# Where the expert weights are kept, what SyncE stores first, and whether GpSimd scatters or gathers first, in a graph network followed by a mixture of experts

## The chip, the cores and the metric

The kernel runs on one core of a Trainium2 chip. The metric is the device time of one execution in microseconds (us), lower is better. Five engines work side by side: TensorE (PE; its weight loads are listed as PEld), VectorE (DVE), ScalarE (ACT), GpSimd (POOL) and SyncE (SP). They meet through semaphores. In this kernel SyncE starts all plain DMAs of the last stage, and GpSimd starts the indirect ones.

## The reference

The input is a graph with 3125 nodes of 256 channels and 53125 edges. A five-layer message network is applied to the normalised rows and added to them; then a mixture of 8 experts is applied to the normalised sum and added again. Cut to what matters here:

```python
x = x + mpnn(layernorm(x), edge_index, edge_attr, ...)      # 5 layers
h = layernorm(x)
logits = h @ Wg + bg + bias                                 # 8 experts
topk_vals, topk_idx = top_k(logits, 2)
w = softmax(topk_vals)                                      # two weights for each node
y[e] = relu(h @ W1[e] + b1[e]) @ W2[e] + b2[e]              # 256 -> 512 -> 256
x = x + sum over the two chosen e of w[e] * y[e]
```

## The kernel before

**Layers.** Nodes lie in 25 tiles of 125 (`NT`, `P`). The adjacency matrix stays in SBUF as fp8 blocks of 500 columns (`at_block(q)`, seven blocks). A layer multiplies its node products `m` with the blocks, first for one half of the channels (groups 0 to 6), then for the other (groups 7 to 13). After group 7 + q of the last layer, block q is not read again. `s_agg` counts the groups, `s_agge` their evictions, `s_tr` the row tiles that TensorE has transposed back (25 for each half of the channels), `s_lo` the row tiles that VectorE has added into the residual `x2`.

**Between the layers and the experts.** TensorE turns `x2` and forms the gate logits, VectorE forms the statistics and picks two experts for each node, ScalarE writes the normalised rows `xn`, SyncE stores them to `xn_dram`. VectorE then sorts the 6250 (node, expert) pairs by expert into tiles of 128 (`TT`), each expert's part filled up to whole tiles. `J` = 56 tiles always suffice; a tile beyond the last used one is a spare tile, whose rows go to the 128 padding rows behind the output. Tables from this: `rowG` (which rows to gather), `rowS` (which output rows to add to), `te` (the expert of a tile), `ts` (how many tiles have to be in memory before a tile may be added).

**The expert loop.** For each tile j, in this order of work: GpSimd gathers its rows from `xn_dram` into one of four buffers (`xtb`, `XB` = 4); TensorE transposes them (`rows`, L1562), ScalarE copies them to SBUF; TensorE multiplies with the up weights (`up`, L1571, 16 matmuls) that VectorE has copied from `w1s` into `w1c` (L1452); ScalarE applies relu; TensorE multiplies with the down weights in `w2s` (`down`, L1581, 8 matmuls); VectorE adds the bias from `b2B` (L1431) and scales with the pair's weight (L1437); GpSimd scatters the result with an accumulating DMA into the output (L1258). The output already holds the residual rows. A node is in two experts' tiles, so the first tile of an expert waits (`s_done`, counted by SyncE) until all tiles of the experts before it have landed. TensorE's order in step j is up of tile j+1, transposes of tile j+2, down of tile j. GpSimd's order is gather of tile j+4, scatter of tile j.

**Memory.** SBUF is laid out by hand in regions that overlap in time. `w1s` and `w2s` take 32 KB a partition each, `xn` 25 KB, `b2B` 8 KB. Before the change `xn` and `b2B` stand in the first adjacency blocks behind the residual, `w1s` where the products `m` were, and `w2s` where the hidden rows `hA` and `hB` were.

**SyncE's queue** runs in the order in which it is written, and each wait in it holds everything behind: residual inputs `x2`, `b2B`, `b1T` (eight DMAs of single values), `w1s`, `w2s`, the two stores of `xn`, the store of `x2` into the output, the zero padding rows; after that it counts landings.

Of the kernel before, what the change touches and what calls it, by code (L numbers as in the profile page):

```python
# [17 lines left out]
N = 3125  # L18
D = 256
E = 53125  # L20
L = 5
# [59 lines left out]
def gnn_ffn_program(nc, x, src, dst, edge_attr, mlp_w, mlp_b, ew1, ew2, bn_g, bn_b,  # L81
                    wg, bg, gbias, w1, b1, w2, b2, out):
    ctx = ExitStack()
    with ctx:
# [186 lines left out]
        assert r.at <= NT * 3 * CQ  # L271
        xn = r("xn", [TT, NT, XW], F32)
        b2B = r("b2B", [128, NE, D], F32)
        b1T = r("b1T", [128, NE, FK], F32)
# [6 lines left out]
        r = Region(hT_at)  # L281
        w2s = r("w2s", [128, NE, FK, D], F32)
        fmv = r("fmv", [P, NT, 2], F32)
# [33 lines left out]
        tsF = r("tsF", [1, J], F32)  # L317
        tsJ = r("tsJ", [1, J], F32)
        ts = r("ts", [1, J], I32)
        assert r.at <= dinvB_at + 2 * 4 * N  # L320
        r = Region(m_at)
        w1s = r("w1s", [128, NE, H, F], F32)
        xtb = r("xtb", [TT, XB, XW], F32)
# [179 lines left out]
        def node_rows(a, lo, hi):  # L503

            return a.rearrange("(t p) d -> p t d", p=P)[lo:hi, :, :]
# [670 lines left out]

        X_STORES = ((0, 13), (13, NT))
        EXP_AT = 10
        GATE, IDS, USED = (bank[4], bank[3]), bank[2], bank[3]
# [23 lines left out]
        def experts_sp(sp):  # L1203

            for n, t in enumerate(range(0, NT, X_PIECE)):

                sp.wait_ge(s_agg, H * NQ * (L - 1) + NQ + n + 1)
                some = slice(t, min(t + X_PIECE, NT))
                for lo, hi in SPANS:
                    sp.dma_start(x2[lo:hi, some, :], node_rows(x, lo, hi)[:, some, :]).then_inc(s_x2[n], 16)  # L1210
            sp.wait_ge(s_agg, L * H * NQ)
            sp.dma_start(b2B[:, :, :], b2.rearrange("(a e) f -> a e f", a=1).to_broadcast([128, NE, D])).then_inc(s_fw, 16)
            with nc.allow_non_contiguous_dma(reason="a few values for each hidden channel"):
                for e in range(NE):
                    sp.dma_start(b1T[:, e, :], b1[e:e + 1, :].rearrange("a (k p) -> p (a k)", p=128)).then_inc(s_fw, 16)

            sp.wait_ge(s_tr, NT * L)
            sp.dma_start(w1s[:, :, :, :].rearrange("p e k f -> p (e k) f"), w1.rearrange("e (k p) f -> p (e k) f", p=128)).then_inc(s_w1, 16)

            sp.wait_ge(s_tr, NT * (L + 1))  # L1220
            sp.dma_start(w2s[:, :, :, :].rearrange("p e k d -> p (e k) d"), w2.rearrange("e (k p) d -> p (e k) d", p=128)).then_inc(s_w2, 16)

            sp.wait_ge(s_wx, 1)
            for a, b in X_STORES:
                sp.wait_ge(s_fn, b)
                sp.dma_start(xn_dram.rearrange("(t p) d -> p t d", p=TT)[:, a:b, :], xn[:, a:b, :]).then_inc(s_xnd, 16)

            sp.wait_ge(s_lo, NT * (L + 2))
            for lo, hi in SPANS:
                sp.dma_start(node_rows(out[0:N, :], lo, hi), x2[lo:hi, :, :]).then_inc(s_res, 16)  # L1230
            sp.wait_ge(s_cst, 1)
            sp.dma_start(out[N:N + TT, :], zt[:, :]).then_inc(s_res, 16)

            sp.sem_inc(s_done, 1)
            for j in range(J):
                sp.wait_ge(s_acc[j % XB], 16 * (j // XB + 1))
                sp.sem_inc(s_done, 1)

        def experts_pool(pool, step):

            pool.wait_ge(s_cst, 2)
            pool.wait_ge(s_agg, H * NQ * L)
            pool.memset(xn[96:TT, :, :], 0.0).then_inc(s_cst, 1)  # L1243
# [8 lines left out]
            def accumulate(j):  # L1252

                before = pool.value_load(ts[0:1, j:j + 1], min_val=1, max_val=J + 1)
                pool.wait_ge(s_done, before)
                pool.wait_ge(s_yb, j + 1)
                pool.sem_inc(s_apart, 1)
                pool.indirect_dma_start(out[:, :], bass.IndirectOffsetOnAxis(ap=rowS[:, j:j + 1], axis=0), ytb[:, j % XB, :], None,  # L1258
                                        compute_op=ALU.add).then_inc(s_acc[j % XB], 16)
# [5 lines left out]
            pool.wait_ge(s_slot, 1)  # L1265
            for j in range(J):
                if j + XB < J:
                    pool.wait_ge(s_xtT, j + 1)
                    pool.wait_ge(s_sel, j + 1)
                    gather(j + XB)  # L1270
                accumulate(j)
            pool.wait_ge(s_done, J + 1)
# [42 lines left out]
        def experts_dve(dve, step, rounded, inverse_root):  # L1315
# [100 lines left out]
            step(dve.tensor_reduce(tsF[:, :], cmpJ[:, 0, :, :], axis=XYZ, op=ALU.add))  # L1416
            step(dve.scalar_tensor_tensor(tsJ[:, :], teF[:, :], NE - 0.5, iotaJ[0:1, :], ALU.is_gt, ALU.mult))
            step(dve.tensor_tensor(tsF[:, :], tsF[:, :], tsJ[:, :], ALU.max))
            step(dve.tensor_scalar(ts[:, :], tsF[:, :], 1.0, None, ALU.add))
# [42 lines left out]
            dve.wait_ge(s_slot, 1)  # L1462
            dve.wait_ge(s_w1, 16)
            weights_of(0, 0, None)
# [9 lines left out]
        def experts_pe(pe):  # L1474
# [79 lines left out]
            pe.wait_ge(s_slot, 1)  # L1554
            pe.wait_ge(s_w1, 16)
            pe.wait_ge(s_w2, 16)
# [688 lines left out]
```

## Time and profile before

| | us |
|---|---|
| median of 3 runs | 1569.53 (1569.2 to 1570.07) |
| the profiled execution | 1569.19 |
| its span, first to last instruction | 1567.5 |
| TensorE busy (matmuls) | 1402.3 (89%) |
| VectorE busy | 718.3 (46%) |
| ScalarE busy | 421.6 (27%) |
| GpSimd busy | 179.4 (11%) |
| mean granted clock of TensorE | 0.948 of full speed |

Rows of a timeline give start and duration in us, engine, line, operation, what it writes and reads, and in brackets how long the engine had been idle and who ended that. SPq is SyncE issuing a DMA. A row of the chain of waits gives start, duration and what the end of the program was waiting for then. A row of windows gives the stretch, its length, the busy time of each engine with its count of instructions, the granted clock, the DMA share and GB/s. Times run from the start of the span.

### The profile page before, as it was taken

The page shows a single profiled execution, that of the slowest core. Times are in us where ns is not written, and L with a number is a line of the kernel's source. Part 1 is how long each engine was busy: PE and PEld are TensorE (multiplying, and loading weights), DVE is VectorE, ACT ScalarE, POOL GpSimd, SP SyncE. Part 2 cuts the span into 40 slices and gives each one's busy share as a digit, 9 for nine tenths or more (in the row PEclk, how much of TensorE's full clock was granted, in tenths as well). Part 3 has the DMA queues.
Part 4 walks back from the last instruction along what each step waited for, and adds up shares of the span by engine and source line. Part 5 has one row for each costly group of instructions (what it writes and reads, how often), then busy time and mean ns, then how long its engine had stood idle before and what let it go on. Part 6 is the DMA issues. An engine that isn't in the chain of part 4 may idle for free.

```text
span 1567.5 us, 25937 instructions
## 1 busy us (share of the span) xinstructions
PE 1402.3 (89%) x9117; PEld 859.2 (55%) x9118; DVE 718.3 (46%) x1713; ACT 421.6 (27%) x1159; POOL 179.4 (11%) x156
## 2 busy tenths in 40 slices
PE   2666468988888999999999999999999998899996
PEld 1655344444444554446444474444644466799995
DVE  6789777777743332313223141221312238444442
ACT  1820344433340330103101040010401025344342
POOL 1000100000000000000000000000000010577774
PEclk9976689999999999999999999999999998999998
DMA  5244000000000000000000000000000329444443
GB/s 118 69 155 172 1 1 1 1 2 1 1 21 1 14 1 1 0 1 14 1 0 0 1 15 0 0 1 7 2 0 11 72 49 326 90 71 70 68 73 44
DMA packets 49739, 58.01 MB, mean 37 GB/s; under 512 B 14432, under 2 KB 41789, under 8 KB 49372
## 3 DMA queue, kind: packets, MB, share of 16 engines
q1 hardware_dynamic: 38876, 41.78, 9.1%
q0 software_dynamic: 10752, 14.74, 6.0%
q8 instruction: 70, 1.15, 0.3%
q14 instruction: 41, 0.34, 0.1%
HBM read 42.42 MB, written 14.09 MB: 36 GB/s over the span
## 4 chain that ended last, share of the span: by engine, by line
PE 80%; DVE 7%; ACT 6%; issue 3%; DMA 2%; DVEq 1%; SPq 1%; POOL 0%; POOLq 0%; ACTq 0%
PE bank L937 43%; PE bank L1027 9%; PE bank L1571 6%; PE bank L1581 6%; PE bank L843 5%; PE bank L2187 4%; ACT at L2055 2%; PE bank L2129 2%; DMA xin<-in_x 1%; PE bank L943 1%; PE bank L2185 1%; DVE ohL L1844 1%; PE bank L1562 1%; ACT xjunk L2002 1%; ACT xjunk L1995 1%
## 5 line engine op out<-in xcount | busy, mean ns | idle before, releaser
L937 PE MATMUL bank<-at,m 125*128 125x500 fp8e4 (+1 forms) x3500 | 688.3, 354 | 7.8 <-issue 4.1
L937 PEld LDWEIGHTS bank<-at,m 125*128 125x128 f16 x3500 | 317.7, 98 | 369.0 <-issue 50.7
L953 DVE SCALAR_TENSOR_TENSOR aggT<-bank,dnL,dinvB 128x500 f32<-128x500 f32 (+1 forms) x56 | 38.2, 682 | 453.8 <-PE bank L943 453.8
L1571 PEld LDWEIGHTS bank<-xtT,w1c 128*128 128x128 f32 x896 | 109.6, 193 | 3.3 <-ACT xtT L1293 0.5
L1571 PE MATMUL bank<-xtT,w1c 128*128 128x128 f32 x896 | 110.0, 276 | 0.1
L1581 PE MATMUL bank<-w2s,h1T 128*128 x448 | 106.0, 380 | 0.0
L1258 POOL DMA_INDIRECT out_rows<-ytb,rowS x56 | 98.0, 1750 | 49.2 <-issue 18.2
L1243 POOL MEMSET xn<- 32x6450 f32 x1 | 5.5, 5473 | 792.8 <-PE bank L943 792.8
L1049 ACT ACTIVATE hB<-aggT,prm 128x500 f32<-128x500 f32 (+1 forms) x28 | 18.7, 667 | 267.1 <-DVE aggT L1099 267.1
L1581 PEld LDWEIGHTS bank<-w2s,h1T 128*128 128x128 f32 x448 | 80.8, 190 | 8.9
L2044 ACT ACTIVATE encI<-bank 125x500 int32<-125x500 f32 x32 | 18.8, 587 | 228.5 <-PE bank L2191 228.4
L2187 PE MATMUL bank<-cnt,ohS 128*128 128x250 bf16 x504 | 75.8, 297 | 0.0
L1951 DVE TENSOR_TENSOR cnt<-iotaK,nowKD 128x2000 bf16<-128x2000 int16 x63 | 75.1, 1192 | 0.0
L1299 ACT ACTIVATE h1T<-bank,b1T 128x128 f32<-128x128 f32 x224 | 64.0, 368 | 27.6 <-issue 23.0
L1250 POOL DMA_INDIRECT xtb<-xn_dram,rowG x56 | 57.2, 1022 | 66.8 <-DVE rowG L1413 45.6
L1027 PE MATMUL bank<-hB,wt 128*128 128x500 f32 (+1 forms) x140 | 64.7, 544 | 0.0
L2185 PE MATMUL bank<-ohD,now 128*12 128x50 bf16 x504 | 25.0, 192 | 44.1 <-DVE ohS L1953 43.5
L869 DVE SCALAR_TENSOR_TENSOR m<-bank,dinvP,m 125x256 f16<-125x256 f32 x100 | 43.0, 478 | 35.5 <-ACT m L864 35.4
L1452 DVE COPY w1c<-w1s 128x1024 f32 x56 | 39.8, 711 | 41.8 <-issue 23.8
L2055 ACT ACTIVATE at<-encB 125x500 fp8e4<-125x500 uint8 (+1 forms) x96 | 57.0, 599 | 0.4 <-DVE encB L1916 0.4
L2185 PEld LDWEIGHTS bank<-ohD,now 128*12 128x12 bf16 x504 | 19.1, 101 | 65.6 <-issue 65.1
L2187 PEld LDWEIGHTS bank<-cnt,ohS 128*128 128x128 bf16 x504 | 47.2, 104 | 11.7
(387 smaller groups left out, 1649.4 us busy)
## 6 DMA issues: line engine op xcount, KB each, us to landing
slrow<-sl_dram SPq DMA_DIRECT2D x26, 512.0 KB, 5.0
w1s<-in_L_ffn_W SPq DMA_DIRECT2D x1, 4096.0 KB, 14.5
w2s<-in_L_ffn_W SPq DMA_DIRECT2D x1, 4096.0 KB, 19.1
xin<-in_x SPq DMA_DIRECT2D x1, 2800.0 KB
out_rows<-x SPq DMA_DIRECT2D x1, 2800.0 KB
x<-in_x SPq DMA_DIRECT2D x2, 1344.0 KB
xn_dram<-xn SPq DMA_DIRECT2D x1, 1677.0 KB, 7.5
dinvB<-dinv_dram SPq DMA_DIRECT2D x1, 1562.5 KB
```

The source lines that it names most:

```text
L843: last = pe.matmul(pair_slot(t), half_in(l, h)[:, t * P:(t + 1) * P], wb[:, l % 2, h, :], start=h == 0 and t % 2 == 0, stop=h == H - 1 and ...
L937: pe.matmul(agg_bank(l, g)[:, 0:w], m[:, s, k, h * 128:(h + 1) * 128], at_block(q)[:, s, :], start=s == 0 and k == 0, stop=False)
L1027: last = pe.matmul(lin_bank(l, j, q)[:, 0:w], weights, src_k, start=k == 0, stop=k == ks[-1])
L1250: pool.indirect_dma_start(xtb[:, j % XB, :], None, xn_dram[:, :], bass.IndirectOffsetOnAxis(ap=rowG[:, j:j + 1], axis=0)).then_inc(s_xt[j ...
L1258: pool.indirect_dma_start(out[:, :], bass.IndirectOffsetOnAxis(ap=rowS[:, j:j + 1], axis=0), ytb[:, j % XB, :], None, compute_op=ALU.add). ...
L1299: last = act.activation(h1T[:, u, k, :], bank[4 + u][:, k * TT:(k + 1) * TT], ACT.Relu, bias=b1T[:, bass.ds(e, 1), k:k + 1].rearrange("p a ...
L1571: last = pe.matmul(bank[4 + u][:, k * TT:(k + 1) * TT], w1c[:, u, h, k * 128:(k + 1) * 128], xtT[:, u, h, :], start=h == 0, stop=h == H - 1)
L1581: last = pe.matmul(bank[6 + u][:, 0:D], h1T[:, u, k, :], w2s[:, bass.ds(e, 1), k, :].rearrange("p a f -> p (a f)"), start=k == 0, stop=k = ...
L1951: dve.tensor_tensor(cnt1[side][:, :, :, :], to_all(iotaK[:, :, :], U // 2), by_pairs(nowKD[:, side, 0, :], GW), ALU.is_equal)
L2055: last = act.activation(at_block(q)[:, field:field + FIELDS * (GROUPS - 1) + 1:FIELDS, a:a + n], byte[:, f, :, 0:n], ACT.Copy, saturate=False,
L2185: pe.matmul(sums_w, now[:, side, 0:12, j], ohD[side][:, j // 2, :, j % 2], start=False, stop=False)
L2187: last = pe.matmul(out_w, ohS[side][:, j // 2, :, j % 2], cnt1[side][:, j // 2, :, j % 2].rearrange("p (g n) -> p g n", g=GROUPS), start=F ...
```

## The change

It has four parts.

1. Memory and loads. `w1s` moves into the adjacency region, behind `x2`, and is loaded in three pieces (experts 0 and 1, 2 to 4, 5 to 7), each when the last layer has used block 2, 3 or 4 for the last time. `w2s` moves to the place of `m` and is loaded after the last aggregation. `xn` and `b2B` move to the place of `hA` and `hB`; so GpSimd's clearing of the padding rows of `xn` waits for all row transposes, and `b2B` is loaded after the last eviction.
2. Stores. SyncE stores the residual rows and the zero padding rows ahead of the two stores of `xn`.
3. Spare tiles. Two VectorE operations go, which had made each spare tile wait for all tiles ahead of it. A spare tile now waits for all tiles of all experts.
4. GpSimd's loop. Scatter j stands ahead of gather j+4.

```diff
         assert r.at <= NT * 3 * CQ
-        xn = r("xn", [TT, NT, XW], F32)
-        b2B = r("b2B", [128, NE, D], F32)
+        w1s_at = r.at
+        w1s = r("w1s", [128, NE, H, F], F32)
...
         r = Region(hT_at)
-        w2s = r("w2s", [128, NE, FK, D], F32)
+        xn = r("xn", [TT, NT, XW], F32)
+        assert r.at >= dinvB_at
+        b2B = r("b2B", [128, NE, D], F32)
...
         r = Region(m_at)
-        w1s = r("w1s", [128, NE, H, F], F32)
+        w2s = r("w2s", [128, NE, FK, D], F32)
...
+        W1_PIECES = ((2, 0, 2), (3, 2, 5), (4, 5, NE))
...
-            sp.wait_ge(s_agg, L * H * NQ)
-            sp.dma_start(b2B[:, :, :], b2.rearrange("(a e) f -> a e f", a=1).to_broadcast([128, NE, D])).then_inc(s_fw, 16)
+            for block, a, b in W1_PIECES:
+                assert w1s_at + 4 * H * F * b <= NT * CQ * (block + 1)
+                sp.wait_ge(s_agg, H * NQ * (L - 1) + NQ + block + 1)
+                sp.dma_start(w1s[:, a:b, :, :].rearrange("p e k f -> p (e k) f"), w1[a:b].rearrange("e (k p) f -> p (e k) f", p=128)).then_inc(s_w1, 16)
             with nc.allow_non_contiguous_dma(reason="a few values for each hidden channel"):
                 for e in range(NE):
                     sp.dma_start(b1T[:, e, :], b1[e:e + 1, :].rearrange("a (k p) -> p (a k)", p=128)).then_inc(s_fw, 16)
 
+            sp.wait_ge(s_agg, L * H * NQ)
             sp.wait_ge(s_tr, NT * L)
-            sp.dma_start(w1s[:, :, :, :].rearrange("p e k f -> p (e k) f"), w1.rearrange("e (k p) f -> p (e k) f", p=128)).then_inc(s_w1, 16)
-
-            sp.wait_ge(s_tr, NT * (L + 1))
             sp.dma_start(w2s[:, :, :, :].rearrange("p e k d -> p (e k) d"), w2.rearrange("e (k p) d -> p (e k) d", p=128)).then_inc(s_w2, 16)
+
+            sp.wait_ge(s_agge, L * H * NQ)
+            sp.dma_start(b2B[:, :, :], b2.rearrange("(a e) f -> a e f", a=1).to_broadcast([128, NE, D])).then_inc(s_fw, 16)
+            sp.wait_ge(s_cst, 1)
+            sp.dma_start(out[N:N + TT, :], zt[:, :]).then_inc(s_res, 16)
+            sp.wait_ge(s_lo, NT * (L + 2))
+            for lo, hi in SPANS:
+                sp.dma_start(node_rows(out[0:N, :], lo, hi), x2[lo:hi, :, :]).then_inc(s_res, 16)
 
             sp.wait_ge(s_wx, 1)
             for a, b in X_STORES:
                 sp.wait_ge(s_fn, b)
                 sp.dma_start(xn_dram.rearrange("(t p) d -> p t d", p=TT)[:, a:b, :], xn[:, a:b, :]).then_inc(s_xnd, 16)
 
-            sp.wait_ge(s_lo, NT * (L + 2))
-            for lo, hi in SPANS:
-                sp.dma_start(node_rows(out[0:N, :], lo, hi), x2[lo:hi, :, :]).then_inc(s_res, 16)
-            sp.wait_ge(s_cst, 1)
-            sp.dma_start(out[N:N + TT, :], zt[:, :]).then_inc(s_res, 16)
...
             pool.wait_ge(s_cst, 2)
-            pool.wait_ge(s_agg, H * NQ * L)
+            pool.wait_ge(s_agge, H * NQ * L)
+            pool.wait_ge(s_tr, NT * (L + 1))
             pool.memset(xn[96:TT, :, :], 0.0).then_inc(s_cst, 1)
...
             for j in range(J):
+                accumulate(j)
                 if j + XB < J:
                     pool.wait_ge(s_xtT, j + 1)
                     pool.wait_ge(s_sel, j + 1)
                     gather(j + XB)
-                accumulate(j)
...
-            step(dve.scalar_tensor_tensor(tsJ[:, :], teF[:, :], NE - 0.5, iotaJ[0:1, :], ALU.is_gt, ALU.mult))
-            step(dve.tensor_tensor(tsF[:, :], tsF[:, :], tsJ[:, :], ALU.max))
             step(dve.tensor_scalar(ts[:, :], tsF[:, :], 1.0, None, ALU.add))
...
-            dve.wait_ge(s_w1, 16)
+            dve.wait_ge(s_w1, 16 * len(W1_PIECES))
...
-            pe.wait_ge(s_w1, 16)
+            pe.wait_ge(s_w1, 16 * len(W1_PIECES))
             pe.wait_ge(s_w2, 16)
```

GpSimd at the start of the expert loop, before: the clearing of `xn`, the four first gathers, then the gather of tile 4 ahead of the scatter of tile 0 (L1250 is a gather, L1254 the reading of `ts`, L1258 a scatter).

```order
L1243 MEMSET xn 32x6450 [waits s_agg,s_cst]
L1250 DMA xtb<-xn_dram,rowG 128x258 [waits s_xnd,s_tab]
L1250 DMA xtb<-xn_dram,rowG 128x258 x3
L1250 DMA xtb<-xn_dram,rowG 128x258 [waits s_xtT,s_sel,s_slot,s_res,s_tab]
L1254 TENSOR_LOAD ts
L1254 ISA x2
L1258 DMA out_rows<-ytb,rowS 3253x256 [waits s_done,s_yb]
L1250 DMA xtb<-xn_dram,rowG 128x258 [waits s_xtT,s_sel]
```

The same place of the changed kernel, where the gather is L1255 and the scatter L1263.

```order
L1248 MEMSET xn 32x6450 [waits s_tr,s_agge,s_cst]
L1255 DMA xtb<-xn_dram,rowG 128x258 [waits s_xnd,s_tab]
L1255 DMA xtb<-xn_dram,rowG 128x258 x3
L1259 TENSOR_LOAD ts [waits s_slot,s_tab,s_res]
L1259 ISA x2
L1263 DMA out_rows<-ytb,rowS 3253x256 [waits s_done,s_yb]
L1255 DMA xtb<-xn_dram,rowG 128x258 [waits s_xtT,s_sel]
```

The first scatter, with its waits for a tile's result and for the residual rows, has moved ahead of the fifth gather, and so for every later pair.

SyncE from the last load of `x2` (named x_156 here) to the end, before.

```order
L1210 DMA x_156<-in_x 13x256
L1212 DMA b2B<-in_L_ffn_b 128x2048 [waits s_agg]
L1215 DMA b1T<-in_L_ffn_b 128x4x1 x8
L1218 DMA w1s<-in_L_ffn_W 128x16x512 [waits s_tr]
L1221 DMA w2s<-in_L_ffn_W 128x32x256 [waits s_tr]
L1226 DMA xn_dram<-xn 128x13x258 [waits s_fn,s_wx]
L1226 DMA xn_dram<-xn 128x12x258 [waits s_fn]
L1230 DMA out_rows<-x_156 112x25x256 [waits s_lo]
L1230 DMA out_rows<-x_156 13x25x256
L1232 DMA out_rows<-zt 128x256 [waits s_cst]
```

And in the changed kernel.

```order
L1212 DMA x_156<-in_x 13x256
L1216 DMA w1s<-in_L_ffn_W 128x4x512 [waits s_agg]
L1216 DMA w1s<-in_L_ffn_W 128x6x512 [waits s_agg] x2
L1219 DMA b1T<-in_L_ffn_b 128x4x1 x8
L1223 DMA w2s<-in_L_ffn_W 128x32x256 [waits s_tr,s_agg]
L1226 DMA b2B<-in_L_ffn_b 128x2048 [waits s_agge]
L1228 DMA out_rows<-zt 128x256 [waits s_cst]
L1231 DMA out_rows<-x_156 112x25x256 [waits s_lo]
L1231 DMA out_rows<-x_156 13x25x256
L1236 DMA xn_dram<-xn 128x13x258 [waits s_fn,s_wx]
L1236 DMA xn_dram<-xn 128x12x258 [waits s_fn]
```

The up weights have moved ahead of all else in three pieces, `b2B` behind the down weights, and the residual's stores ahead of those of `xn`.

## Rows read from the trace of the kernel before

**Rows 1.** The page, chain that ended last, by engine, whole span.

```profile
PE 80%; DVE 7%; ACT 6%; issue 3%; DMA 2%; DVEq 1%; SPq 1%; POOL 0%; POOLq 0%; ACTq 0%
```

**Rows 2.** Chain of waits, 1327 to 1382: start, duration, what.

```profile
1333.02 8.14 DMA xtb<-xn_dram,rowG
...
1341.30 0.67 PE bank L1562 x2
...
1342.51 4.79 PE bank L1571 x32
...
1379.11 1.78 PE bank L1571 x16
```

**Rows 3.** Timeline, expert loop, 1377 to 1389: tile 8 and the tiles around it.

```profile
1377.22 1.89 PE L1581 MATMUL bank<-w2s,h1T 128*128 x8
...
1379.91 0.35 DVE L1437 TENSOR_SCALAR ytb<-ytt,wS 128x256 f32<-128x256 f32 x1 [0.22 <-DVE ytt L1431]
...
1380.95 1.89 PE L1581 MATMUL bank<-w2s,h1T 128*128 x8
1381.10 1.92 POOL L1258 DMA_INDIRECT out_rows<-ytb,rowS  x1 [0.96 <-issue]
...
1383.32 0.99 POOL L1250 DMA_INDIRECT xtb<-xn_dram,rowG  x1 [0.30 <-issue]
...
1384.46 0.38 PE L1562 MATMUL bank<-ident,xtb 128*128 128x128 f32 x2
...
1384.68 1.89 PE L1581 MATMUL bank<-w2s,h1T 128*128 x8
```

**Rows 4.** Scatters: ns min/median/max, 1352 to 1545; group with mean, 1360 to 1540.

```profile
L1258 POOL DMA_INDIRECT out_rows<-ytb,rowS x52: 1583/1694/2078, 1351.1 to 1541.6; - x52
...
L1258 POOL DMA_INDIRECT out_rows<-ytb,rowS x49 | 86.3, 1761 | 32.2 <-issue 16.6 <-PE bank L1562 8.4 <-DVE wS L1445 7.3
```

**Rows 5.** Gathers into xtb, 1340 to 1420: from issue to landing.

```profile
DMA to landing us min/median/max: 2.8/2.8/3.7
```

**Rows 6.** Timelines of GpSimd (first, last of eight wide spacings) and VectorE (last result).

```profile
1388.46 1.96 POOL L1258 DMA_INDIRECT out_rows<-ytb,rowS  x1 [0.46 <-issue]
...
1393.51 1.59 POOL L1258 DMA_INDIRECT out_rows<-ytb,rowS  x1 [1.79 <-DVE wS L1445]
...
1552.49 1.55 POOL L1258 DMA_INDIRECT out_rows<-ytb,rowS  x1 [1.97 <-DVE ytb L1437]
...
1553.08 0.57 DVE L1437 TENSOR_SCALAR ytb<-ytt,wS 128x256 f32<-128x256 f32 x1
1557.03 1.55 POOL L1258 DMA_INDIRECT out_rows<-ytb,rowS  x1 [2.98 <-SPq L1237]
```

**Rows 7.** Timeline of SyncE, 1262 to 1350.

```profile
1282.24 6.52 SPq L1215 DMA_DIRECT2D b1T<-in_L_ffn_b  x8
...
1321.39 10.18 SPq L1230 DMA_DIRECT2D out_rows<-x  x2
```

**Rows 8.** Windows: length, busy PE, PEld, DVE, ACT, POOL, granted clock, DMA share, GB/s.

```profile
1297.00:1305.00 8.00, 7.96 (x72) 7.73 (x71) 5.06 (x41) 4.34 (x12) 0.00 (x0) 0.91 1.07 374
...
1313.00:1317.00 4.00, 2.00 (x11) 1.07 (x12) 3.79 (x26) 3.99 (x10) 0.00 (x0) 1.00 0.32 103
...
1341.00:1345.00 4.00, 3.57 (x17) 3.19 (x18) 0.70 (x4) 0.73 (x2) 0.94 (x1) 0.57 0.14 37
```

**Rows 9.** Timeline of VectorE, 1262 to 1350.

```profile
1298.79 0.15 DVE L1323 TENSOR_TENSOR gbS<-gbr 125x8 f32<-125x8 f32 x1
...
1305.58 0.32 DVE L1714 RECIPROCAL frs<-fsd 125x25 f32<-125x25 f32 x1 [3.38 <-ACT fsd L1282]
...
1333.51 0.20 DVE L1417 SCALAR_TENSOR_TENSOR tsJ<-teF,iotaJ 1x56 f32<-1x56 f32 x1
...
1333.98 0.25 DVE L1419 TENSOR_SCALAR ts<-tsF 1x56 int32<-1x56 f32 x1
...
1337.40 0.69 DVE L1452 COPY w1c<-w1s 128x1024 f32 x1 [1.98 <-issue]
```

## What the change will do to the time

> **What bounds the kernel now.** I read the chain of waits first, then the timeline of the expert stage, then SyncE's queue and the windows. The chain is 80% TensorE [rows 1], so the question is where the edited instructions touch TensorE, and there are three such places. (a) The entry of the expert stage: the chain goes through the first gather of token rows, which takes 8.14 us from GpSimd's issue until TensorE can transpose, and the two up products behind it take 4.79 us for 32 matmuls [rows 2]. In the loop 16 of them take 1.78 us [rows 2]. (b) The loop over 56 tiles: between two down products (1377.22 and 1380.95, then 1384.68) there are 3.73 us with TensorE never idle; everything else is hidden behind it [rows 3]. (c) The end: the last scatter starts 2.98 us late because it waits for landings that SyncE counts [rows 6].
>
> **The loop.** This edit decides the time. Today GpSimd issues gather j+4 and then scatter j. After the change it issues scatter j first and gather j+4 behind it, so the gather inherits everything the scatter waits for: the down product of tile j, VectorE's two operations on it, and the scatter's own instruction. Each gather stands one tile later than now. The slack is in rows 3. Tile 8's down product starts at 1377.22, VectorE has its result at 1380.26, the scatter runs from 1381.10 to 1383.02 and the next gather starts at 1383.32. Before the change that is gather 13; its landing takes 2.8 us [rows 5], so it is there at 1386.12, and TensorE transposes tile 13 at 1388.19, 3.73 us behind tile 12. That is 2.1 us of slack. Shifted by one tile the same place holds gather 12, and tile 12 is transposed at 1384.46: 1.7 us too late. So the slack of today is smaller than the 3.73 us that the change takes from it.
>
> Late gathers feed back, since TensorE's next results are what the next scatters wait for. The loop is: down product j, result j, scatter j, gather j+4, transposes of tile j+4, down product j+2. Its length from the start of one down product to the start of the next but one is: 3.04 us to the end of the result (1377.22 to 1380.26), 0.84 to the scatter [rows 3], 1.76 for a scatter (mean of 49) [rows 4], 0.30 to the gather [rows 3], 2.8 to its landing [rows 5], 0.14 until TensorE starts (landing at 1333.02 + 8.14, transposes at 1341.30) [rows 2], 0.22 from transposes to the down product [rows 3]. The sum is 9.10 us. TensorE's own work for these two tiles is 7.46 us. So two tiles cost 1.64 us more, and two such loops (even and odd tiles) run side by side. Scatters 0 to 51 each have a gather behind them, so each loop closes 26 times: 26 x 1.64 = **+42.6 us**. Ends: the shortest scatter (1.58) [rows 4] gives 8.92, so 26 x 1.46 = +38; with the 0.22 us off that VectorE waits between its two operations here, but not on every tile [rows 3], 8.70 and +32. The longest scatter (2.08) and a landing of 3.2, between median and longest (3.7) [rows 5], give 9.82, so +61. I take the means because the pattern of scatter and gather in turn is the same in both kernels.
>
> The Trainium skill, in "DMA: Bandwidth & Descriptors", section "Anatomy of one DMA — SWDGE (gpsimd) path", has a fit of 2.0 us plus bytes over 436 GB/s for a GpSimd DMA. For 128 rows of 1032 bytes that is an estimate of 2.3 us, which would make the loop 8.6 us, the cost 26 x 1.14 = 30 us, and the time about 1595; the rows show 2.8 us, so the measured value stands.
>
> **Boundaries between experts.** Where the next expert begins, a scatter waits until all earlier ones have landed. Two scatters are then 5.05 us apart instead of 3.73 (1388.46 and 1393.51) [rows 6]; spacings over 4.5 us occur eight times in the trace, seven of them at a first tile of an expert. In the slower loop scatters are 4.55 us apart on average, alternating 3.73 and 5.37. A boundary that falls on a short spacing delays one of the two loops by up to 1.3 us, one on a long spacing costs nothing. Six of them have a gather behind them: half on short ones, shared between two loops, 6 x 1/2 x 1.3 / 2 = about **+2 us**, ends 0 and 4.
>
> **The entry.** SyncE now issues the stores of residual rows right after the last addition to them, and the stores of normalised rows behind them. Today the residual stores are issued from 1321.39 to 1331.57 [rows 7], and the first gather, issued at 1333.02, sits 8.14 us behind them [rows 2] where others land in 2.8 [rows 5]. Without them it lands near 1336. What is late next is VectorE's copy of the first up weights, 1337.40 to 1338.09. It moves earlier by the two operations on spare tiles that go (1333.51 to 1333.98, 0.47 us) [rows 9], to 1337.62. So the first up product starts near 1337.7 instead of 1342.51: 4.8 us. It also starts without the long pause that now stands before it. The granted clock was 0.57 from 1341 to 1345 [rows 8], mostly the lower of its two levels (1.2 GHz), and the 32 matmuls took 4.79 us against 2 x 1.78. That is another 1.2 us if the clock stays up. Together **-6.0 us**; -4.4 if it doesn't, and the first down product starts near 1341.5.
>
> **What is hidden.** Up weights: three pieces into adjacency blocks already used, during the last aggregation, when the queue is nearly free; nobody waits for them before 1337. Down weights: issued behind the last aggregation instead of behind the last row transposes, and first read by the first down product. The bias rows b2 now stand behind the down weights, and VectorE's wait for all small parameters stands ahead of its gate bias at 1298.79 [rows 9]. 5.2 MB at 374 GB/s [rows 8] from about 1283.5 take 14 us, so they land near 1297.5. If they are late, all of VectorE's routing work is queued behind that wait, but VectorE idles 3.38 us for ScalarE's square root before 1305.58 [rows 9], so the first 3 us cost nothing. The eight slow b1 loads, now ahead of the weights on SyncE's queue for 6.52 us [rows 7], go under the aggregation. GpSimd's clearing of the padding rows moves to about 1296.5, still 5 us ahead of the first reader. I take 0 for all of this, with -0.5 to +1.5 as bounds.
>
> **Spare tiles.** Unchaining them gives nothing: the chain shows in one place only, at the very last scatter (start 1557.03, result ready at 1553.65) [rows 6]. Were there two or more spare tiles, scatter 54 would wait for landings as well; it starts at 1552.49, released by VectorE's result. So tile 55 is the only spare one, and even unchained it waits for all 55 real tiles, tile 54 included. What goes is the 0.47 us counted above.
>
> **Sum.** The profiled execution took 1569.19 us (span 1567.5); the median of the runs shown is 1569.53, so I add to the profiled one and see no difference that matters. 1569.2 - 6.0 + 42.6 + 2 = **1608 us**.
>
> **Rivals.** (1) The loop absorbs the shift and only the entry counts: 1569.2 - 6.0 = 1563. Place: between scatter j and the transposes of tile j+4. It decides at a loop of 7.46 us instead of 9.10, so 1.64 us would have to vanish, for instance a gather that lands 1.2 us after its start. For it: TensorE waits for no gather in the loop today. Against: the shortest landing in the loop is 2.8 us [rows 5], and the scatter can't start before its result. 5%. (2) The pauses bring the clock down. TensorE would stand still 1.6 us in 9.1, and if the transposes and the down product behind each pause ran at the lower level (1.95 us more a loop, by the doubling that the up products show from 1.78 to 2.4 with a mean clock of 0.57), the loop is 11.05 us and the time 1569.2 - 4.4 + 26 x 3.59 = 1658. For it: the 0.57 behind the long wait [rows 8]. Against: from 1313 to 1317 TensorE was busy only 2.00 of 4.00 us and the granted clock was 1.00 [rows 8], the full level of 2.4 GHz. The Trainium skill ("TensorE: Matmul & The Clock Gate", section "Part 1: The HAM clock gate (the "warmup" mystery)") says that an idle array falls to half rate, 1.2 GHz, and sustained work lifts it again; that is this rival's mechanism, and the row of 1313 to 1317 shows a stretch with pauses that left the clock up. 4%. (3) A smaller or larger loop than 9.10, by the ends above: inside the range.
>
> **How the numbers follow.** The forecast with its ends has 90%: low 1569.2 - 6.5 + 32 = 1595, high 1569.2 - 4.4 + 61 + 4 = 1630. I leave the low end and cut the high one, where every term would have to be at its longest at once, to 1626; with both rivals outside, that leaves out less than 2 in 10. A measurement of this kernel tells about 0.2% (3 us) from no change. Slower: the forecast and rival 2, 0.94. Within 0.2%: 0.01, for a loop that keeps just enough delay to eat the entry's gain. Faster: rival 1, 0.05.
>
> **What would show it.** In the changed kernel, TensorE idle ahead of the transposes of nearly every second tile, released by the landing of a gather, some 43 us in all; down products 9.1 us apart over two tiles; the first gather landing in about 3 us; the first down product near 1341.5; the last scatter still waiting for SyncE. I am wrong if TensorE shows no such waits, if the granted clock in the loop falls below 1.00, or if VectorE is held at the gate bias beyond 1302.

## The result and the profile after

The changed kernel takes 1637.43 us (median of 4 runs, 1634.01 to 1641.50); the kernel before took 1569.8 us beside it (1569.2 to 1570.66). The ratio is 1.043, with a 95% interval of 1.0414 to 1.0447: slower by 68 us. The forecast was 1608 us with a range of 1595 to 1626, so the direction was right and the loss was 29 us larger than forecast, outside the range. The profiled execution took 1638.43 us, with a span of 1636.7. One of the 12 executions of the fifth experiment's kernel took 2418.38 us at a granted clock of 0.559; the median of that kernel counts it, the ratio doesn't.

The page of the changed kernel gives this chain (compare [rows 1]), and below it two of the costliest groups (line, engine, operation, count | busy us, mean ns | idle before and its releaser):

```profile
PE 73%; DVE 7%; DMA 7%; ACT 6%; issue 5%; DVEq 1%; SPq 1%; POOL 0%; POOLq 0%; ACTq 0%
...
L1584 PE MATMUL bank<-w2s,h1T 128*128 x448 | 115.1, 402 | 20.0 <-issue 20.0
L1263 POOL DMA_INDIRECT out_rows<-ytb,rowS x56 | 99.1, 1769 | 122.8 <-issue 94.1
```

TensorE's share of the chain has gone from 80% to 73%, and the landings of DMAs hold 7% of it. L1565 holds the transposes of gathered rows, L1584 the down product, L1574 the up product. TensorE's waits (engine and line, what it waited for: us in total, times, longest) name two things where the loop of before had no wait at all:

```profile
PE bank L1565 <- DMA xtb<-xn_dram,rowG: 31.7, 29, 2.5
PE bank L1584 <- issue: 20.0, 38, 0.8
```

The first is the late gather that the prediction describes. The second it doesn't have: 38 times TensorE stood ahead of a down product for "issue", that is without a releaser that the profile shows. The chain of waits through the entry and the first turn of the loop (start us, duration us, what) shows both; [rows 2] is the same place before:

```profile
1334.86 2.76 DMA xtb<-xn_dram,rowG
1337.62 0.04 issue
1337.66 0.44 PE bank L1565 x2
1338.10 3.57 PE bank L1574 x32
1341.67 0.22 PE bank L1565 x2
1341.89 1.73 PE bank L1584 x8
1343.62 1.78 PE bank L1574 x16
...
1347.49 2.73 DMA xtb<-xn_dram,rowG
1350.22 0.04 issue
1350.27 0.44 PE bank L1565 x2
1350.70 0.42 issue
1351.12 1.99 PE bank L1584 x8
```

The entry came as forecast: the first gather, issued at 1333.36, landed after 3.0 us instead of 8.14, the first up products took 3.57 us instead of 4.79, and the first down product started at 1341.73 instead of 1347.36. The first row of this chain is the second gather, issued at 1334.86; the first gather stands outside it:

```profile
1333.36 1.20 POOL L1255 DMA_INDIRECT xtb<-xn_dram,rowG  x1 [30.07 <-DVE rowG L1418]
DMA to landing us min/median/max: 3.0/3.0/3.0
```

The gather behind the dots is gather 4, the first that GpSimd issues behind a scatter. Behind it the transposes take 0.44 us in the chain (0.22 where nothing waited), then come 0.42 us of "issue", then a down product of 1.99 us. From its first to its last instruction a down product takes 1.89 us elsewhere [rows 3]; the chain's 1.73 leaves out what overlaps the transposes.

I averaged the seven terms of the prediction's loop over its 52 closings in the trace of after:

| term of the loop (us) | predicted | measured, mean | with the early read (third experiment) |
|---|---|---|---|
| start of down j to end of result j | 3.04 | 3.17 | 3.10 |
| to scatter j | 0.84 | 0.91 | 0.92 |
| scatter j | 1.76 | 1.78 | 1.77 |
| to gather j+4 | 0.30 | 0.30 | 0.30 |
| landing of gather j+4 | 2.80 | 2.96 | 2.94 |
| to the transposes | 0.14 | 0.43 | 0.15 |
| start of transposes to start of down j+2 | 0.22 | **0.76** | 0.27 |
| loop | 9.10 | 10.32 | 9.44 |

26 x (10.32 - 7.46) = +74 us, less the entry's 6, is the 68 us measured.

### The profile page after: what moved, and what is told of

Its sections match the earlier page's. It is cut to its first block, busy times and chain, and to the rows that moved or that the text cites. A ratio compares the mean times of both kernels' runs of the same rounds, so it can differ in the third digit from the quotient of the medians.

```text
span 1636.7 us, 25937 instructions
## 1 busy us (share of the span) xinstructions
PE 1423.9 (87%) x9117; PEld 864.0 (53%) x9118; DVE 719.6 (44%) x1711; ACT 421.6 (26%) x1159; POOL 179.0 (11%) x156
## 4 chain that ended last, share of the span: by engine, by line
PE 73%; DVE 7%; DMA 7%; ACT 6%; issue 5%; DVEq 1%; SPq 1%; POOL 0%; POOLq 0%; ACTq 0%
PE bank L938 41%; PE bank L1028 8%; PE bank L1584 6%; DMA xtb<-xn_dram,rowG 5%; PE bank L844 4%; PE bank L2190 3%; PE bank L1574 3%; ACT at L2058 2%; DMA xin<-in_x 1%; PE bank L2132 1%; PE bank L944 1%; PE bank L1565 1%; PE bank L2188 1%; DVE ohL L1847 1%; ACT xjunk L2005 1%
## 5 line engine op out<-in xcount | busy, mean ns | idle before, releaser
L1584 PE MATMUL bank<-w2s,h1T 128*128 x448 | 115.1, 402 | 20.0 <-issue 20.0
L1263 POOL DMA_INDIRECT out_rows<-ytb,rowS x56 | 99.1, 1769 | 122.8 <-issue 94.1
L1574 PEld LDWEIGHTS bank<-xtT,w1c 128*128 128x128 f32 x896 | 110.5, 194 | 3.2
L1574 PE MATMUL bank<-xtT,w1c 128*128 128x128 f32 x896 | 110.4, 277 | 0.0
L1584 PEld LDWEIGHTS bank<-w2s,h1T 128*128 128x128 f32 x448 | 83.7, 197 | 39.3 <-issue 29.3
L1434 DVE TENSOR_TENSOR ytt<-bank,b2B 128x256 f32<-128x256 f32 x56 | 23.8, 424 | 119.2 <-PE bank L1584 119.2
L1298 ACT ACTIVATE xtT<-bank 128x256 f32<-128x256 f32 x56 | 21.5, 384 | 185.5 <-PE bank L1565 185.5
L1255 POOL DMA_INDIRECT xtb<-xn_dram,rowG x56 | 55.8, 996 | 46.8 <-DVE rowG L1418 30.1
```

The source lines that it names most:

```text
L1255: pool.indirect_dma_start(xtb[:, j % XB, :], None, xn_dram[:, :], bass.IndirectOffsetOnAxis(ap=rowG[:, j:j + 1], axis=0)).then_inc(s_xt[j ...
L1574: last = pe.matmul(bank[4 + u][:, k * TT:(k + 1) * TT], w1c[:, u, h, k * 128:(k + 1) * 128], xtT[:, u, h, :], start=h == 0, stop=h == H - 1)
L1584: last = pe.matmul(bank[6 + u][:, 0:D], h1T[:, u, k, :], w2s[:, bass.ds(e, 1), k, :].rearrange("p a f -> p (a f)"), start=k == 0, stop=k = ...
```

## The experiments

Line numbers move by a few from kernel to kernel; the names of the tiles don't. The transposes read `xtb`, down products read `w2s`, up products `w1c`.

**1. Gather first again.**

```diff
             for j in range(J):
-                accumulate(j)
                 if j + XB < J:
                     pool.wait_ge(s_xtT, j + 1)
                     pool.wait_ge(s_sel, j + 1)
                     gather(j + XB)
+                accumulate(j)
```

> The changed kernel with one edit: GpSimd issues gather j+4 ahead of scatter j again, as before the change. Theory (the order alone costs the time, the other parts of the change bring only the earlier entry): the gathers again have 2.1 us of slack, TensorE waits for none of them, two tiles take 7.46 us, and what is left is the entry. The first down product stood at 1341.73 us instead of 1347.36, 5.6 us earlier, in an execution that ran 1.28 us behind the other since 465 us, ahead of all edited code; so 5.6 to 6.9 us less than the kernel before: 1569.5 - 6.3 = 1563 us, 1562 to 1564. Rival (the moved weight loads or stores cost something in the loop too): over 1566 us, and the loop's two tiles longer than 7.46 us.

Measured: 1564.53 us against 1570.45 (ratio 0.9963, 0.9949 to 0.9978), 5.9 us faster than the kernel before. Two tiles take 7.49 us, and in a window of the loop TensorE is never idle (window, length, busy us and instructions of PE, PEld, DVE, ACT and POOL, granted clock, DMA share, GB/s):

```profile
1400.00:1420.00 20.00, 20.00 (x141) 18.89 (x140) 9.18 (x26) 8.63 (x29) 15.31 (x12) 1.00 0.43 67
```

That is 0.5 us above the interval expected, and far from the rival. What follows: the three other parts of the change together are worth some 6 us, and the order of scatter and gather turns that into a loss of 68.

**2. The order alone, on the kernel before.**

```diff
             for j in range(J):
+                accumulate(j)
                 if j + XB < J:
...
                     gather(j + XB)
-                accumulate(j)
```

> The kernel before with one edit: scatter j ahead of gather j+4, nothing else of the change. Theory: the whole loss comes from this order. In the changed kernel two tiles took 10.32 us against 7.46, 26 times, which is +74 us; so 1569.5 + 74 = 1644 us, 1638 to 1650. By the loop as it was sized in the prediction (9.10 us) it would be 1569.5 + 43 + 2 = 1614 us. Rival (part of the loss comes from the moved weights, stores or the unchained tile): under 1630 us.

Measured: 1644.01 us (ratio 1.0463, 1.0447 to 1.0480), as the theory has it. It is 6.6 us above the changed kernel, which is the entry's gain that it lacks: the two effects add. In its trace the loop takes 10.16 us, 26 x 2.70 = 70 us; this execution was also 4.4 us behind the kernel before at its first down product (1351.74), so the order costs 70 to 74 us. Its waits are those of after:

```profile
PE bank L1562 <- DMA xtb<-xn_dram,rowG: 31.9, 27, 5.2
PE bank L1581 <- issue: 20.4, 38, 0.7
```

**3. TensorE reads the expert's number earlier.** Each down product picks its weights by a number that TensorE loads from `te` into a register. In `down` that load stands behind the wait of `rows`; the edit puts it ahead.

```diff
-            def down(j, u, free):
-                e = pe.value_load(te[0:1, bass.ds(j, 1)], min_val=0, max_val=NE - 1)
+            def expert(j):
+                return pe.value_load(te[0:1, bass.ds(j, 1)], min_val=0, max_val=NE - 1)
+
+            def down(j, u, free, e):
...
                     if not (last_group and k == XB - 1):
                         up(j + 1, 1 - u)
+                    e = expert(j)
                     if not (last_group and k >= XB - 2):
                         n = k + 2
                         rows(j + 2, u, n % XB, 16 * (g + n // XB + 1))
-                    down(j, u, None if first and k < 2 else j - 1)
+                    down(j, u, None if first and k < 2 else j - 1, e)
```

> The changed kernel with one edit: TensorE reads the expert's number for down product j ahead of its wait for the gathered rows of tile j+2 instead of behind it; what it multiplies stays the same, and so does GpSimd's order. Theory: the 0.5 to 0.85 us in which TensorE waits for nothing that the profile shows, between the transposes behind a late gather and the down product, is this register load, which used to run ahead under TensorE's queue and now stands behind a blocked wait. Then the stretch from transposes to down product goes back from 0.76 to about 0.22 us, and the time falls by 26 x 0.5 to 26 x 0.7: 13 to 19 us, to 1619 to 1625 us. Rival (it is the restart of the weight loads or of the array after a pause, which comes whatever stands ahead): no change, 1634 to 1641 us.

Measured: 1613.92 us (ratio 1.0270, 1.0247 to 1.0293), 23.5 us less than the changed kernel: the theory, by more than I gave it. The chain at the same place as above has no "issue" between transposes and down product:

```profile
1347.40 2.82 DMA xtb<-xn_dram,rowG
1350.22 0.04 issue
1350.26 0.44 PE bank L1565 x2
1350.70 1.76 PE bank L1586 x8
```

The load itself stands in the rows of TensorE's sequencer (PEldq: line, operation, count: duration in ns, minimum/median/maximum, first and last start in us). The first row has all 56 loads of after. The others are the place above: the load starts at 1350.3, together with the transposes, and its last part, a check of the number's bounds, at 1350.8; the down product starts at 1351.12:

```profile
L1579 PEldq TENSOR_LOAD <-te x56: 297/302/578, 1339.7 to 1617.0; - x56
...
L1579 PEldq TENSOR_LOAD <-te x1: 302/302/302, 1350.3 to 1350.3; - x1
L1579 PEldq FUSED_REGOPS  x1: 151/151/151, 1350.6 to 1350.6; - x1
L1579 PEldq SEQ_ASSERT  x1: 18/18/18, 1350.8 to 1350.8; - x1
```

In the first experiment, where nothing waits, such a load starts at 1352.0, 2 us ahead of its down product:

```profile
L1579 PEldq TENSOR_LOAD <-te x1: 297/297/297, 1352.0 to 1352.0; - x1
...
1353.98 1.89 PE L1584 MATMUL bank<-w2s,h1T 128*128 x8
```

So it ran ahead there for free, and after the change it can't. In the third experiment TensorE's list of waits in the loop has none but that for the gathers (36.1 us, 41 times). The table's last column shows where the surplus over 13 to 19 us came from: not only the 0.49 us from transposes to down product, but another 0.28 us from landing to transposes. My reading: while TensorE stands ahead of one loop's down product, rows of the other loop lie landed behind it, and a shorter restart shortens that too. The tenth experiment bears it out: with a load back at the old place this stretch is 0.38 us again, against 0.15.

**4. Eight buffers.** Gather j+8 behind scatter j, with the order of the change (cut; the buffers' new places are left out).

```diff
-XB = 4
+XB = 8
...
+            pool.wait_ge(s_res, 48)
             for j in range(XB):
                 gather(j)
-            pool.wait_ge(s_res, 48)
```

> The changed kernel with eight buffers of token rows and of results instead of four, so that GpSimd issues scatter j and behind it gather j+8 (eight gathers ahead of the first scatter); the order scatter before gather stays. The buffers lie where other data is already dead; a branch that these inputs do not take shares its semaphores to make room for the new ones. Theory (the order costs only because it makes a gather late, by a loop of four tiles): a gather now has four tiles more, 4 x 3.73 = 14.9 us, against some 3.7 us that the order takes; no waits of TensorE for gathers, two tiles 7.46 us, and the time that of the order gather first: 1562 to 1565 us. Rival (a scatter ahead of a gather slows GpSimd's queue or the transfers themselves, whatever the lead): over 1580 us.

Measured: 1563.18 us (ratio 0.9955, 0.9940 to 0.9971); two tiles 7.46 us, rows landed 13 us ahead of their transposes, no wait of TensorE for a gather. The same order of instructions costs nothing once the gather leads by eight: it was the lateness alone, not a scatter in the gather's way.

**5. Gather first, but the residual rows stored last again.**

```diff
-            sp.wait_ge(s_cst, 1)
-            sp.dma_start(out[N:N + TT, :], zt[:, :]).then_inc(s_res, 16)
-            sp.wait_ge(s_lo, NT * (L + 2))
-            for lo, hi in SPANS:
-                sp.dma_start(node_rows(out[0:N, :], lo, hi), x2[lo:hi, :, :]).then_inc(s_res, 16)
 
             sp.wait_ge(s_wx, 1)
...
+            sp.wait_ge(s_lo, NT * (L + 2))
+            for lo, hi in SPANS:
+                sp.dma_start(node_rows(out[0:N, :], lo, hi), x2[lo:hi, :, :]).then_inc(s_res, 16)
+            sp.wait_ge(s_cst, 1)
+            sp.dma_start(out[N:N + TT, :], zt[:, :]).then_inc(s_res, 16)
```

> The kernel with gather j+4 ahead of scatter j (the first experiment, 1564.5 us) with one more edit: the stores of zero and residual rows stand behind the stores of normalised rows again, as before the change. Theory (the gain of the entry comes from these stores being out of the first gather's way): the first gather again takes about 8 us to land instead of 2.9, the first down product stands some 5 us later, and the time is that of the kernel before, 1569 to 1571 us. Rival (the gain comes from the earlier weights or from the two operations on spare tiles): it stays at 1563 to 1566 us.

Measured: 1571.06 us (ratio 1.0008, 0.9996 to 1.0020). The first gather is slow again, and so are the up products behind it:

```profile
1332.83 8.03 DMA xtb<-xn_dram,rowG
...
1342.09 5.00 PE bank L1575 x32
```

Without the new order of the stores the gain of the entry is gone. The moved weights and the two operations that went gain nothing by themselves that can be measured (by the interval the time is 0.6 us less to 3.1 us more than before).

**6. Gather first, with the early read.** The edits of the first and third experiments together.

> The kernel with gather j+4 ahead of scatter j (the first experiment, 1564.5 us) with TensorE's read of the expert's number ahead of its wait for the gathered rows, the edit that took 23 us from the changed kernel. Theory (that read costs only behind a blocked wait, and here no wait blocks): no change, 1562 to 1567 us, and 0.22 us from transposes to down product as in the first experiment. Rival (the earlier read shortens each tile by itself): 56 x 0.2 us or more, under 1555 us.

Measured: 1563.68 us (ratio 0.9956, 0.9941 to 0.9972), no different from the first experiment; 0.22 us from transposes to down product in both. Where no wait blocks TensorE, the read costs nothing that can be measured, at either place.

**7. Eight buffers, gather first.**

> The kernel with eight buffers of token rows and results, with gather j+8 ahead of scatter j instead of behind it. Theory (with eight tiles of lead the order is without effect): the same as with the scatter first, 1562 to 1565 us. Rival (a scatter ahead of a gather still costs or brings something): more than 3 us away from 1563.

Measured: 1562.67 us (ratio 0.9959, 0.9944 to 0.9974) against 1563.18 with the scatter first: the order is without effect at this lead.

**8 and 9. A pause between scatter and gather.** On the kernel of the third experiment, to see how often a delay there counts (the second run has `0:3` instead of `0:6`).

```diff
                 accumulate(j)
                 if j + XB < J:
+                    pool.memset(xn[96:TT, 0:6, :], 0.0).then_inc(s_cst, 1)
+                    pool.wait_ge(s_cst, 4 + j)
                     pool.wait_ge(s_xtT, j + 1)
```

> The kernel with scatter j ahead of gather j+4 and the early read of the expert's number (1613.9 us), with a clearing of 6 x 258 unused elements on each of 32 partitions on GpSimd between each scatter and the gather behind it. The trace of the changed kernel has such a clearing of 25 x 258 elements in 5.47 us, so one of 6 x 258 takes an estimated 1.3 us. Theory (scatter and gather stand in two loops side by side, each closed 26 times): 26 x 1.3 = +34 us, 1648 us, and two tiles 1.3 us longer. Rival (each scatter and gather pair counts for itself, 52 times): +68 us, 1682 us. Rival (GpSimd is not in the loop, TensorE's restart is): under 1625 us.

> As the run before it (scatter, clearing, gather; early read of the expert's number), with half the clearing: 3 x 258 elements. There the gathers stood 2.26 us behind the scatters on average instead of 0.30, and the loop was 2.75 us longer, with a granted clock of 0.91 in most of it; here the clearing takes an estimated half of 1.98 us, so the gather stands 1.0 us later. Theory (26 closed loops, each lengthened by what stands in it): 26 x 1.0 = +26 us where the clock stays at 1.00, 1640 us, and the surplus of the run before was the clock: with more falls of it here up to 1655. Rival (each of the 52 pairs counts): 52 x 1.0 = +52 us, 1666 us or more with the clock at 1.00.

Measured: 1689.75 us with six rows of clearing, 1655.71 us with three (ratios 1.0755 and 1.0533). Neither hit the number expected, mainly because the pauses were longer than I had estimated. In the run with three (start us, duration us, engine, line, operation, idle before it and its releaser):

```profile
1398.66 1.59 POOL L1263 DMA_INDIRECT out_rows<-ytb,rowS  x1 [0.30 <-issue]
...
1404.22 1.82 POOL L1263 DMA_INDIRECT out_rows<-ytb,rowS  x1 [1.40 <-DVE ytb L1442]
1405.47 1.34 POOL L1274 MEMSET xn<- 32x774 f32 x1
1407.63 0.99 POOL L1255 DMA_INDIRECT xtb<-xn_dram,rowG  x1 [0.82 <-POOL xn L1274]
```

The clearing takes 1.34 us and its signal another 0.82, so the gather starts 1.59 us behind the scatter's end instead of 0.30; on average over the loop it is 1.61, that is 1.31 us more. 26 x 1.31 = 34 us, where 41.8 were measured; 52 x 1.31 = 68 is ruled out. So the model of two loops, each closed 26 times, holds. By the terms of the table this loop takes 11.04 us instead of 9.44. Of the 1.60 us more, 1.31 are the pause, 0.13 stand between result and scatter, 0.09 between down product and result, and 0.07 in the others. The 0.13 is GpSimd: 18 of 51 scatters start 0.30 us behind the gather ahead of them, as at 1398.66, in the third experiment none. The 0.09 goes with TensorE's clock: 7 of the first 52 down products take over 2.3 us, there 2. Windows of 200 us in the loop, of the third experiment, then with three and with six rows of clearing:

```profile
1400.00:1600.00 200.00, 170.50 (x1087) 152.42 (x1086) 77.02 (x209) 63.60 (x209) 115.52 (x83) 0.98 0.35 55
```
```profile
1400.00:1600.00 200.00, 152.69 (x946) 136.95 (x947) 67.11 (x182) 55.79 (x184) 129.77 (x111) 0.96 0.31 48
```
```profile
1400.00:1600.00 200.00, 146.66 (x839) 130.95 (x838) 62.34 (x161) 49.43 (x163) 136.32 (x98) 0.89 0.28 43
```

With six rows the clearing takes 1.98 us and the gather stands 1.96 us later than without. The time is near the 1682 us of the rival only because that was worked out with a pause of 1.3 us; with 1.96 it gives 52 x 1.96 = 102 us and 1716. The loops give 26 x 1.96 = 51 us of the 75.8 measured. Their length is 12.19 us, 2.75 more than in the third experiment: beside the pause, 0.39 us from down product to result, where the mean down product takes 2.31 us instead of 1.98, and 0.34 from result to scatter, where 25 of 51 scatters follow the gather ahead by 0.30 us. This execution was also 3.8 us behind at the first down product. So the surplus here is partly the clock, rival 2 of the prediction (26 x 0.39 = 10 us), and as much GpSimd's own time (26 x 0.34 = 9 us); no run changes one of them alone.

**10. A second read at the old place.** The kernel of the third experiment, with a load of the same number, used by no product, at the head of `down`.

```diff
             def down(j, u, free, e):
+                pe.value_load(te[0:1, bass.ds(j, 1)], min_val=0, max_val=NE - 1)
```

> The kernel with scatter first and the early read of the expert's number (1613.9 us), with a second read of that number, which no product uses, back at the old place: behind the wait for the gathered rows, ahead of the down product. Theory (a read costs by standing behind a blocked wait on TensorE's queue, whoever uses the value): back to the changed kernel's 1634 to 1641 us, and the stretch from transposes to down product back to 0.76 us. Rival (the early read gained by something else, or only the product that uses the value waits for it): it stays under 1622 us.

Measured: 1633.76 us (ratio 1.0406, 1.0377 to 1.0434), 0.2 us short of the interval expected by the theory and far from the rival; 0.70 us from transposes to down product. In its chain the "issue" is back:

```profile
1349.76 0.44 PE bank L1565 x2
1350.19 0.41 issue
1350.61 1.99 PE bank L1587 x8
```

A read behind a blocked wait costs about the same whether or not a product uses the value: 19.8 us here, 23.5 us where the product uses it.

## Why the prediction was right or wrong

**The entry: right.** Forecast -6.0 us; experiment 1 measures -5.9 and experiment 5 pins it on the stores. The price of 1.2 us for the clock held too: the first up products took 3.57 us (2 x 1.78 forecast). One stop on the way is another: the prediction lets VectorE's copy of the up weights come last, but both copies were done at 1337.26, and the second gather, landed at 1337.62, released TensorE. That the first up product still starts near the 1337.7 of the forecast (1337.94) is luck. The -4.4 for a clock that stays down should be -4.8 by the prediction's own terms.

```profile
1335.81 1.45 DVE L1455 COPY w1c<-w1s 128x1024 f32 x2 [0.61 <-issue]
```

**The hidden parts: right.** The bias rows landed later than the 1297.5 that I gave them, near 1300.9, and the gate bias waited for them, but the square root behind it still left slack (rows of VectorE as in [rows 9], there 3.38 us):

```profile
1300.92 0.17 DVE L1328 TENSOR_TENSOR gbS<-gbr 125x8 f32<-125x8 f32 x1 [0.86 <-DMA b2B<-in_L_ffn_b]
...
1306.13 0.32 DVE L1717 RECIPROCAL frs<-fsd 125x25 f32<-125x25 f32 x1 [1.78 <-ACT fsd L1287]
```

**Spare tiles: right.** The last scatter still waits for SyncE, as in [rows 6]:

```profile
1626.19 1.55 POOL L1263 DMA_INDIRECT out_rows<-ytb,rowS  x1 [3.05 <-SPq L1241]
```

**The loop: the mechanism right, its size wrong.** The seven terms, two loops side by side and 26 closings are what the runs show (experiments 2, 4, 8, 9). The step that failed is the term "0.22 from transposes to the down product [rows 3]". It was read at a place where TensorE was never idle, and there its register load cost nothing that shows. Behind a late gather the load stands after the blocked wait and is paid in the open: 0.76 us, 0.54 more, of which the load's own row takes 0.30 us and what hangs on it (register operations, the check of bounds) the rest. The Trainium skill ("DMA: Bandwidth & Descriptors", section "Latency and other measured facts") has a floor of some 600 ns for a `tensor_load`. The trace doesn't agree: the 56 rows of TENSOR_LOAD take 0.30 us in the median and 0.58 at the longest, and the measurement stands. I had the code of `down` before me and looked for waits in it, not for an instruction that had been free only because TensorE was behind. By experiment 3 this one misjudged instruction is worth 23.5 us, with what it delays in the other loop: the term "0.14 until TensorE starts", read at the entry, was 0.43 (26 x 0.29 = 8 us), and falls to 0.15 with the load out of the way. Without the load the kernel takes 1614 us, inside the range. The rest are small: a landing of 2.96 us where I took the median of 2.8 ([rows 5] show 3.7 as the longest; a loop pays the mean), 26 x 0.16 = 4 us, and the result's 0.13, 3 us.

**Boundaries: +2 us forecast.** They are part of the means above. The stretch from result to scatter exceeds the forecast by 0.07 us, 26 x 0.07 = 1.8 us; no run tests it apart.

**Rival 1** (the loop absorbs the shift) needed a gather that lands 1.2 us after its start; the shortest landing in any trace is 2.7 us. **Rival 2** (the clock) happened a little. The granted clock was 1.00 in most of the loop, but fell to the lower level four times, for example here (windows of 4 us, columns as above):

```profile
1428.00:1432.00 4.00, 2.00 (x13) 1.53 (x12) 1.42 (x4) 0.54 (x2) 3.08 (x3) 0.91 0.46 70
1432.00:1436.00 4.00, 4.00 (x19) 3.39 (x18) 0.70 (x2) 0.99 (x4) 0.33 (x1) 0.67 0.28 58
1436.00:1440.00 4.00, 4.00 (x31) 3.79 (x30) 1.83 (x6) 1.53 (x5) 2.79 (x2) 1.00 0.19 16
```

The down product in it, behind a pause of 1.48 and 0.52 us, took 3.56 us instead of 1.99:

```profile
1431.46 3.56 PE L1584 MATMUL bank<-w2s,h1T 128*128 x8 [0.52 <-issue]
...
1442.89 1.99 PE L1584 MATMUL bank<-w2s,h1T 128*128 x8 [0.61 <-issue]
```

Four falls at 1.6 us are some 6 of the 74 us at most; the rival's 1.95 us in every loop is not there. The doubling that set the rival's price isn't in the row that the prediction names: from 1.78 to 2.4 is a factor of 1.35, and the fall above shows 1.8 (3.56 and 1.99). The row that it set against the rival, 1.00 from 1313 to 1317, didn't last either: in the trace of after the same stretch, with a pause of 4.59 us where the kernel before has 2.03, shows 0.78:

```profile
1313.00:1317.00 4.00, 1.54 (x5) 0.83 (x6) 3.79 (x29) 3.99 (x9) 0.00 (x0) 0.78 0.00 0
```

The Trainium skill, in the passage that the prediction weighs ("TensorE: Matmul & The Clock Gate", section "Part 1: The HAM clock gate (the "warmup" mystery)"), says that an idle array falls to half rate. The four falls, each behind a pause, and the 0.89 of experiment 8 agree with it; most pauses of this loop left the clock at 1.00 all the same.

**What would show it.** I had asked for waits of some 43 us for gathers; there are 31.7 us and another 20.0 us of "issue" beside them. The second row was the mark of the mis-sized term. Of the signs of being wrong that the prediction lists one came, a granted clock below 1.00 in the loop, but only in the four falls.

## What to carry to other kernels

Before an engine is made to wait where it never waited, go through every instruction behind the new wait up to its next real work, register loads included: those that ran ahead for free now stand on the path. In a loop that closes on itself, take means and not medians, and multiply by how often the loop closes. A prefetch moved behind a write-back needs as much more lead as that write-back waits for: with eight buffers the order cost nothing that can be measured, with four it cost 70 to 74 us.

## What the runs showed of the hardware

- A register load on TensorE takes 0.30 us in its own row (median of 56). Behind a blocked wait, with the check of its value, it shows as 0.2 to 0.8 us of "issue" ahead of the product (38 times, 20.0 us), and the product itself takes 1.99 us instead of 1.89. With no wait ahead of it (experiments 1 and 6) the load cannot be seen in the time at all.
- Pauses of about the same length can lower TensorE's clock or leave it: 1.48 and 0.52 us ahead of the fall at 1431, while the pause ahead of the down product at 1442.89 (1.31 and 0.61 us) left it at 1.00. With longer pauses falls were more frequent: a mean of 0.98 in experiment 3, 0.96 and 0.89 in experiments 9 and 8.
- A clearing on GpSimd doesn't shrink in proportion to its size: on 32 partitions 774 elements each took 1.33 us, 1548 took 1.98, 6450 took 5.47, and a gather that waits for its signal started 0.82 us after its end.
